# Attention fills by halves: queries, keys, stack and ten score fills of batch b+2 move from the phase boundary into the phase

## What is computed

```python
x = x + tanh(g_xattn[0]) * retention(layernorm(x), ctx)       # 2 heads of 128, group norm, gate
x = x + tanh(g_ffn[0])   * top1_of_8_experts(layernorm(x))    # inner width 176
x = x + tanh(g_xattn[1]) * attention(layernorm(x), ctx)       # the change is here
x = x + tanh(g_ffn[1])   * ffn_2_to_4(layernorm(x))           # inner width 1024, keeps 2 of 4
```

```python
q = (Q @ w_q.T).reshape(B, S, 8, 4, 8); k = (K @ w_k.T).reshape(B, S, 8, 8); v = likewise
scores = einsum("bnghd,bmgd->bnghm", q, k) / sqrt(8)      # masked: padding and m > n
out = einsum("bnghm,bmgd->bnghd", softmax(scores), v).reshape(B, S, D) @ w_o.T + b_o
```

## Time and profile before

| | |
|---|---|
| median of three runs | 403.8 us (402.51 to 404.14) |
| the profiled execution | 402.7 us |
| its span, first to last instruction | 400.6 us |
| PE busy | 340.5 us (85%) |
| VectorE (DVE) busy | 214.3 us (54%) |
| ScalarE (ACT) busy | 160.0 us (40%) |
| GpSimd (POOL) busy | 98.4 us (25%) |
| mean granted TensorE clock | 0.936 |

### The profile page before, as it was taken

How to read it: one execution, slowest core, us unless ns; L and a number is a source line. 1 busy time by engine, 2 the same in 40 slices (tenths; PEclk the granted TensorE clock), 3 DMA queues, 4 the chain that set the end, 5 groups by cost and what they waited for, 6 DMA issues and landing times.

```text
span 400.6 us, 4557 instructions
## 1 busy us (share of the span) xinstructions
PE 340.5 (85%) x1471; PEld 205.7 (51%) x1477; DVE 214.3 (54%) x509; ACT 160.0 (40%) x336; POOL 98.4 (25%) x148
## 2 busy tenths in 40 slices
PE   2999775609999838989799989997979989999997
PEld 1485564405666426545453646364453534444886
DVE  4144985601322257879626944693141349778921
ACT  2543221204333123144892877286795223333000
POOL 7103553430000256401440335044343001000000
PEclk9999997558999765999999999998999999999999
DMA  7996000134111114500000000000000000000011
GB/s 204 383 420 144 1 13 2 41 123 152 42 52 41 52 40 136 245 1 5 2 7 0 2 7 2 0 1 9 0 2 0 0 2 0 0 1 2 24 42 39
DMA packets 13879, 22.40 MB, mean 56 GB/s; under 512 B 2033, under 2 KB 11249, under 8 KB 13042
## 3 DMA queue, kind: packets, MB, share of 16 engines
q1 hardware_dynamic: 13090, 20.03, 14.7%
q0 software_dynamic: 768, 2.10, 1.6%
HBM read 15.83 MB, written 6.03 MB: 55 GB/s over the span
## 4 chain that ended last, share of the span: by engine, by line
PE 57%; DVE 20%; ACT 8%; issue 7%; POOL 4%; DMA 3%; another core or an unknown queue 1%; SPq 0%; DVEq 0%; ACTq 0%; POOLq 0%
PE bank L229 43%; DVE mx L1156 9%; ACT region L880 5%; PE bank L438 5%; PE bank L406 3%; DVE stats L951 2%; POOL x_sorted L697 2%; POOL rstd L673 2%; PE bank L242 1%; DVE x_sb L991 1%; PE bank L409 1%; DMA x_sb<-in_x_dram 1%; PE bank L452 1%; PE bank L486 1%; PE bank L236 1%
## 5 line engine op out<-in xcount | busy, mean ns | idle before, releaser
L1156 DVE TENSOR_REDUCE mx<-bank 128x2 f32<-128x512 f32 (+1 forms) x96 | 59.7, 682 | 14.1 <-PE bank L409 7.8
L880 ACT ACTIVATE region<-bank,padcol 128x512 f32<-128x512 f32 x96 | 60.9, 702 | 12.6 <-PE bank L229 11.6
L735 POOL TENSOR_SCALAR_AFFINE_SELECT region<-region 128x1024 f32<-128x1024 f32 x32 | 35.1, 1097 | 94.6 <-ACT region L880 94.2
L229 PE MATMUL bank<-xT,e_gu 128*128 128x512 f32 x128 | 57.6, 594 | 0.5 <-ACT xT L752 0.5
L229 PE MATMUL bank<-qst,kblk 128*128 128x512 f32 x96 | 46.0, 506 | 1.6 <-ACT region L880 0.7
L406 PE MATMUL bank<-kblk,qst 128*128 128x512 f32 x96 | 43.4, 475 | 1.7 <-DVE mx L1156 0.9
L229 PEld LDWEIGHTS bank<-xT,e_gu 128*128 128x128 f32 x128 | 23.3, 190 | 25.1 <-issue 24.3
L669 POOL TENSOR_SCALAR veps<-mv 128x1 f32<-128x1 f32 x40 | 11.4, 285 | 73.9 <-DVE mv L953 73.5
L752 ACT ACTIVATE xT<-bank 128x256 f32<-128x256 f32 x32 | 12.4, 387 | 42.4 <-PE bank L236 42.2
L409 PE MATMUL bank<-causb,identb 128*128 128x256 bf16 (+1 forms) x90 | 28.3, 314 | 0.0
L229 PE MATMUL bank<-e_down,region 128*128 128x256 f32 x128 | 27.8, 379 | 0.0
(11 more groups left out here) (155 smaller groups left out, 545.3 us busy)
## 6 DMA issues: line engine op xcount, KB each, us to landing
e_gu<-in_e_gu_dram SPq DMA_DIRECT2D x2, 1408.0 KB, 12.6
x_sorted<-zero SPq DMA_DIRECT2D x1, 1920.0 KB, 10.1
y_sorted<-region SPq DMA_DIRECT2D x15, 128.0 KB, 1.7
x_sb<-in_x_dram SPq DMA_DIRECT2D x4, 256.0 KB, 4.2
ctxT<-in_ctxT_dram SPq DMA_DIRECT2D x2, 512.0 KB, 7.5
e_down<-in_e_down_dram SPq DMA_DIRECT2D x1, 1024.0 KB, 14.3
region<-x_sorted SPq DMA_DIRECT2D x1, 1024.0 KB, 7.6
e_gu<-in_f_gate_dram SPq DMA_DIRECT2D x1, 1024.0 KB, 4.8
```

The source lines that it names most:

```text
L229: return pe.matmul(dst, lhsT, rhs, start=first, stop=last)
L735: pool.affine_select(out=block, in_=block, compare_op=ALU.is_ge, fill=0.0, base=0, pattern=[[0, 2], [0, PER_GROUP], [1, P]], channel_multi ...
L880: taken(act.activation(dst, src.rearrange("p (h n) -> p h n", n=SEQ - mt * P), ACT.Exp, bias=padcol[:, key:key + 1], scale=float(HD) ** -0 ...
L1156: taken(dve.reduce_max(mx[:, b % 2, nt, quads, q, hg], src, AX), "sa")
```

## The change

`QUERIES_AT` goes from 10 to 2, so that queries stand at slots 2, 4 and 6. `keys` and `query_stack` are cut in pieces, and a new `ahead` puts the key projection in slot 8, the value projection in slot 10, ks0 in slot 11 and the first two stack fills in slot 12. The first ten score fills of batch b+2 stand in slots 14 to 23. At the boundary are left ks1, two stack fills, the four values, and one score fill behind each of the first two. kp and vp go to bank 7 and ks0 to bank 6 instead of "wide"; two stack fills go to "max", two to "exp". Ahead of phase 0 the stack of batch 1 moves into slots 16 to 22 of the score loop, and `neg_turn(0)` behind the third score fill of batch 1, on two banks. The ScalarE wait before a stack copy is by halves. Nothing is computed otherwise.

```diff
-QUERIES_AT = 10
+QUERIES_AT = 2
+KEYS_AT = 8
+STACK_AT = 12
+NEXT_AT = 14
+LATE_FILLS = 2
@@ PE
+            def ahead(b, n):
+
+                if n == KEYS_AT:
+                    key_projection(b, "tok1")
+                elif n == KEYS_AT + 2:
+                    value_projection(b, "tok1")
+                elif n == STACK_AT - 1:
+                    key_half(b, 0, "turn1")
+                elif n == STACK_AT:
+                    stack_piece(b, 0, "max")
+                    stack_piece(b, 1, "max")
...
-            query_stack(0, "main")
+            for piece in range(4):
+                stack_piece(0, piece, "main")
             for n in range(24):
                 scores(0, n)
                 queries(1, n)
-            query_stack(1, "exp")
-            neg_turn(0, "turn1")
+                if n >= 16 and n % 2 == 0:
+                    stack_piece(1, (n - 16) // 2, "exp")
             for n in range(LEAD):
                 scores(1, n)
+                if n == 2:
+                    neg_turn(0, ("turn1", "tok1"))
             for b in range(BATCH):
                 for n in range(24):
                     if b + 1 < BATCH and n + LEAD < 24:
                         scores(b + 1, n + LEAD)
+                    if b + 2 < BATCH and 0 <= n - NEXT_AT < LEAD:
+                        scores(b + 2, n - NEXT_AT)
                     weights(b, n)
                     if b >= 1 and n % 2 == 1:
                         finish(b - 1, n // 2)
                     if b + 2 < BATCH:
                         queries(b + 2, n)
+                        ahead(b + 2, n)
...
                 if b + 2 < BATCH:
-                    keys(b + 2, "wide")
-                    query_stack(b + 2, "wide")
+                    key_half(b + 2, 1, "turn1")
+                    stack_piece(b + 2, 2, "exp")
+                    stack_piece(b + 2, 3, "exp")
 
                 for i in range(4):
                     values(b, i)
-                    for n in range(i * LEAD // 4, (i + 1) * LEAD // 4):
-                        if b + 2 < BATCH:
-                            scores(b + 2, n)
+                    if b + 2 < BATCH and i < LATE_FILLS:
+                        scores(b + 2, LEAD - LATE_FILLS + i)
@@ ScalarE
+            def stack_piece(b, piece):
+                q, h = divmod(piece, 2)
+                src = filled(act, "qs", 4 * b + piece).rearrange("p (h n) -> p h n", h=2)
+                if b >= 2:
+                    act.wait_ge(sem("sb_ready"), 24 * (b - 2) + 12 * (q + 1))
...
                     if b + 2 < BATCH:
                         queries(b + 2, n)
+                        ahead(b + 2, n)
...
                 if b + 2 < BATCH:
-                    keys(b + 2)
-                    query_stack(b + 2)
+                    stack_piece(b + 2, 2)
+                    stack_piece(b + 2, 3)
                 value_turn(b)
@@ VectorE
+                    if b + 2 < BATCH and 0 <= n - NEXT_AT < LEAD:
+                        row_maxima(b + 2, n - NEXT_AT)
...
                         queries(b + 2, n)
+                        if n == KEYS_AT + 1:
+                            key_low(b + 2)
...
                 if b + 2 < BATCH:
-                    key_low(b + 2)
                     spread_keys(b + 2)
+                    for n in range(LEAD - LATE_FILLS, LEAD):
+                        row_maxima(b + 2, n)
```

More of the change, by code:

```diff
@@ L355, in queries, with stack_piece, key_projection @@
                 ready(ins, "qp")
-            def query_stack(b, one):
+            def stack_piece(b, piece, one):
                 s = b % 2
+                q, h = divmod(piece, 2)
+                dst = acquire(pe, "qs", 4 * b + piece, one)
                 pe.wait_ge(sem("qp_taken"), b + 1)
[L361 to L373, removed]
+                for e in range(2):
+                    hg = 2 * h + e
+                    mm(dst[:, e * SEQ:(e + 1) * SEQ], selr[:, hg * P:(hg + 1) * P], qhi[:, s, q, :], True, False)
+                    ins = mm(dst[:, e * SEQ:(e + 1) * SEQ], selr[:, (4 + hg) * P:(5 + hg) * P], qlo[:, s, q, :], False, True)
+                ready(ins, "qs")
+            def key_projection(b, one):
                 dst = acquire(pe, "kp", b, one)
@@ L377, in keys, with value_projection @@
                 for t in range(KT):
-                    ins = mm(dst[:, 0:SEQ], wk[:, t, :], ctxT[:, t, seq], t == 0, t == KT - 1)
+                    ins = mm(dst[:, 0:SEQ], wk[:, t, :], ctxT[:, t, b * SEQ:(b + 1) * SEQ], t == 0, t == KT - 1)
                 ready(ins, "kp")
+            def value_projection(b, one):
                 dst = acquire(pe, "vp", b, one)
@@ L385, in keys, with key_half @@
                 ready(ins, "vp")
-                if b == 0:
+            def key_half(b, q, one):
+                if b == 0 and q == 0:
                     pe.wait_ge(sem("sel_made"), 2)
                     pe.wait_ge(sem("padrow_made"), 1)
+                dst = acquire(pe, f"ks{q}", b, one)
                 pe.wait_ge(sem("kp_taken"), b + 1)
-                for q in range(HALVES):
-                    dst = acquire(pe, f"ks{q}", b, one)
-                    mm(dst[:, 0:SEQ], selr[:, (8 + q) * P:(9 + q) * P], khl[:, s, :], True, False)
-                    ready(mm(dst[:, 0:SEQ], padselr[:, :], padrow[:, seq], False, True), f"ks{q}")
+                mm(dst[:, 0:SEQ], selr[:, (8 + q) * P:(9 + q) * P], khl[:, b % 2, :], True, False)
+                ready(mm(dst[:, 0:SEQ], padselr[:, :], padrow[:, b * SEQ:(b + 1) * SEQ], False, True), f"ks{q}")
+            def keys(b, one):
+                key_projection(b, one)
+                value_projection(b, one)
+                for q in range(HALVES):
+                    key_half(b, q, one)
+            def ahead(b, n):
[8 more added lines that the diff above has]
+                    stack_piece(b, 1, "max")
             def scores(b, n):
@@ L410, in scores, with neg_turn @@
                                 skip_group_check=True), "sa")
-            def neg_turn(b, kind):
+            def neg_turn(b, kinds):
                 s = b % 2
                 for nt in range(2):
-                    dst = acquire(pe, "nmT", 2 * b + nt, kind)
+                    dst = acquire(pe, "nmT", 2 * b + nt, kinds[nt])
                     pe.wait_ge(sem("nm_made"), 2 * b + nt + 1)
@@ L534, in _ @@
                     if n == NEGATE_AT and b + 1 < BATCH:
-                        neg_turn(b + 1, "turn1")
+                        neg_turn(b + 1, ("turn1", "turn1"))
                 if b + 2 < BATCH:
-                    keys(b + 2, "wide")
-                    query_stack(b + 2, "wide")
+                    key_half(b + 2, 1, "turn1")
+                    stack_piece(b + 2, 2, "exp")
+                    stack_piece(b + 2, 3, "exp")
                 for i in range(4):
                     values(b, i)
-                    for n in range(i * LEAD // 4, (i + 1) * LEAD // 4):
-                        if b + 2 < BATCH:
-                            scores(b + 2, n)
+                    if b + 2 < BATCH and i < LATE_FILLS:
+                        scores(b + 2, LEAD - LATE_FILLS + i)
             def half_piece(stage, w, g, j):
@@ L789, in _, with key_high @@
             act.activation(r_s[:, 3, :], r_s[:, 2, :], ACT.Exp).then_inc(sem("vexp"), 1)
-            def keys(b):
-                s = b % 2
+            def key_high(b):
                 src = filled(act, "kp", b)
@@ L796, in keys, with value_rows @@
                     act.wait_ge(sem("ks1_ready"), b - 1)
-                act.activation(khl[:, s, :], src[:, 0:SEQ], ACT.Copy).then_inc(sem("k_high"), 1)
+                act.activation(khl[:, b % 2, :], src[:, 0:SEQ], ACT.Copy).then_inc(sem("k_high"), 1)
+            def value_rows(b):
                 src = filled(act, "vp", b)[:, 0:2 * GROUPS * HD].rearrange("p (k g d) -> p k g d", k=2, g=GROUPS)
@@ L803, in keys, with spread_half @@
                 taken(ins, "vp")
+            def spread_half(b):
+                s = b % 2
                 if b < 2:
@@ L811, in keys, with ahead @@
                 taken(ins, "ks0")
+            def keys(b):
+                key_high(b)
+                value_rows(b)
+                spread_half(b)
+            def ahead(b, n):
+                if n == KEYS_AT:
+                    key_high(b)
+                elif n == KEYS_AT + 2:
+                    value_rows(b)
+                elif n == STACK_AT - 1:
+                    spread_half(b)
+                elif n == STACK_AT:
+                    stack_piece(b, 0)
+                    stack_piece(b, 1)
             def queries(b, n):
@@ L822, in queries @@
                 act.activation(qhi[:, s, :, :], src, ACT.Copy).then_inc(sem("q_high"), 1)
[L824 to L832, removed]
+            def stack_piece(b, piece):
+                q, h = divmod(piece, 2)
+                src = filled(act, "qs", 4 * b + piece).rearrange("p (h n) -> p h n", h=2)
+                if b >= 2:
```

(14 more changed lines are left out.)

## The result

The changed kernel takes 410.1 us (median of four runs, 409.8 to 410.5) against 404.0 us before; the ratio is 1.0155, with a 95% interval of 1.0129 to 1.0182. It is slower by 6.1 us, where I had forecast 3.3. The sign was right and the stated range held the time; the size of the change was nearly twice the forecast.

A forecast was written before the change was run, and what follows sets the result against it. PE (busy 85% of the span) was taken as the bound, with only its waits to win. Terms -2.1 + 0.7 + 3.2 + 0.7 + 0.8 = +3.3 took the profiled 402.7 to 406.0 us, median 407; range 399 to 412.

The forecast's parts named there:

- Ahead of phase 0: Before batch 1's first reduction: VectorE's idle 2.09 us goes, as stack fills move into the score loop; -2.1 us.
- Phase 0, slots: In phase 0's slots, PE waits 1.5 (key projection), 0.6 (value projection), 2.85 (slot 14), 1.15 (slot 15's turn); through at 26.15.
- Boundaries and phase 3: At the ends of phases 0 to 2, fills wait for banks still in use, including phase 3's first weight fill; 5.4 us.
- seven meetings: Boundary waits for a bank still in use: 0.75, 0.75, 0.3, 1.05, 1.05, 0.75 and 0.7 us.
- ten waits counted for phase 1: PE waits in phase 1's slots and boundary, put at 10.1 us; with 31.9 of work, 42.0 against 38.8, +3.2.
- The clock: Thin PE stretches before and behind slot 14 in phases 0 and 1 lower the granted clock; 0.4 us each, +0.8.
- The 3.4: Clock cost in phases 0 and 1 if it falls in both, 1.7 us each, in place of 0.8.
- Rival B: The clock falls in phases 0 and 1, and slower fills delay ScalarE some 1 us; median 410.7 us, chance 0.13.
- Rival A: PE's room is filled as meant, slot waits cost nothing, bank meetings are covered; median 395.4, or 399 by half; chance 0.2.
- Rival C: Losses and gain cancel: boundary meetings cost only half, 2.7 of 5.4 us, and the clock holds; median 403.6, chance 0.22.

The follow-up runs named there:

- kernel with fixed banks: The changed kernel with the value fills put on fixed banks that no neighbouring fill needs; 403.4 us, ratio 0.9999 to the kernel before.
- banks 6 and 7: Changed kernel with fixed value banks, key projection moved to bank 6 and slot 15's two turned maxima on banks 6 and 7; 400.0 us, ratio 0.9900.

## Why the prediction was right in sign and wrong in size

- *Ahead of phase 0*, -2.1: measured -2.4. Right in place; it needs both edits there.
- *Phase 0, slots*: the waits of 1.5, 0.6, 2.85 and 1.15 came as 1.15, 0.41, 2.45 and 0.72 of PE idle, which leaves out the weight loads and modelled tails; by starts, slot 14 came 0.1 from where it was put. Following the streams held to 0.1 us in 18.
- *Boundaries and phase 3*, 5.4 in sum: measured 5.6. All seven meetings are in the trace, each in its place. The working from the counters alone was enough. (The ten waits counted for phase 1 add up to 10.2 and not 10.1.)
- *The clock* is the step that failed. I wrote: "Bounds: nothing, or 3.5 us at 1.2 GHz in each phase [...] 1.7 each. I take 0.4 each, near the low end, since no thin stretch of phases 0 and 1 lost the clock before". It measured 2.6 and 2.2, outside even the upper bound, against 0.8 for both. Two errors. The reason given was worth nothing: the thinnest 2.6 us of phases 0 and 1 before (197.7 to 200.3) had PE busy 1.2, while the wait that I had just derived left it 0.17 in as long a stretch. And the 3.5 us were the length of one fall in phase 2; here each lasted some 7. The price for a length was right: low stretches of some 3.5 us cost 1.6 in phase 0 and 1.0 in phase 1, under the bound of 1.7. What sets the length is open: with the same order in phase 1 it was 7 us in one profile of the changed kernel and 3.5 in the other.
- The rule that I cited, "TensorE: Matmul & The Clock Gate" of the Trainium skill, section "A second HAM failure mode: psum-queue depth-cycling", has the clock fall in both phases, and it did. Its cause is not borne out: it speaks of small idle times between groups of matmuls, and the kernel with eight matmuls in slot 14's wait cycles through the same banks, keeps the idle times of the boundary (0.72 and 0.71 us) and kept full clock in both phases. Here it is the one long wait. The 3.4 was my own working for two falls of 3.5 us, not the page's.
- Rival B (the clock falls in both phases, 410.7 us against 410.1 measured) is what happened, and I gave it 0.13. Its number came out by some luck: it took 3.4 for the clock and 1 for a later ScalarE, where the clock alone cost 4.8. Rival A was wrong as it stood: the waits inside the slots were real. Rival C was wrong too; the boundary cost all that was counted.

Sum by the measured terms: -2.4 (lead) + 5.6 (banks) + 4.8 (clock) = 8.0. With the span's 7.8 that leaves -0.2 for all that the new order does inside the slots at full clock. The kernel with fixed banks shows that directly: its phases, from weight fill to weight fill, take 34.3 and 39.3 us against 34.9 and 38.8. Moving the work into the slots was by itself worth nothing, since the waits of the chain queries, keys, stack and score fill took the room that the boundary gave up. With two of these waits taken away and the clock kept, phase 0 up to the value fills falls from 27.2 to 24.1 us.

## What to carry to other kernels

When fills move from one rotation of banks to another, count the turns of every rotation that shares those banks: who lies where at the seam is fixed by the counts, can be read off without a run, and cost 5.6 us here. Where a change leaves TensorE a new wait like this one (2.5 us, ahead of dense work), price the fall of its clock by the work that follows, at half pace, and don't take it as unlikely because the old order never had such a stretch. Work that fits in the wait costs nothing and may give time back: 1.9 us of unread matmuls did in the wait of 2.5 us, and did not in slot 14 of phase 2, where PE waits 1.4 us and their bank was not free. I would expect real work in that place to be better; no run here has it.

## What I had not expected of the hardware

The granted clock went from 1.0 to 0.5 about 1.5 us after the wait had ended (score fill at 201.1, fall at 202.6), in the middle of dense work, and stayed low for some 7 us. With banks 6 and 7 it fell 0.4 us after the wait (201.2 and 201.6) and stayed low for some 3.5. It is no fixed function of the instructions: the kernel with fixed banks issues the same slots, and held full clock in its profiled execution, with single times from 400.7 to 405.4. And 3.8 us of extra matmuls made a kernel 3.4 us faster (400.0 to 396.7).
